# One GNN and mixture-of-experts layer: earlier and later places for sends, combines and a release, and padding written behind each expert's last token

## The reference

```python
x = x + gnn(layernorm(x), src, dst, edge_weight)      # x: 3125 nodes x 256
x = x + ffn(layernorm(x))
# gnn: support = x @ weight; out = segment_sum(support[src] * edge_weight, dst) + bias   (53125 edges)
# ffn, per token: logits = x @ Wg + bg over 8 experts; the best 2, softmax over the two logits;
#   out = sum over the two experts e of w_e * (gelu(x @ W1[e] + b1[e]) @ W2[e] + b2[e])   (256 -> 1024 -> 256)
```

## Time and profile before

| what | value |
|---|---|
| runs | 1106.56, 1114.02, 1115.84 us |
| profiled execution | 1100.59 us, span 1098.9 us |
| mean granted TensorE clock | 0.871 of full speed |
| PE busy / POOL busy / DVE busy / ACT busy | 780.1 / 601.0 / 491.4 / 354.1 us |
| DMA | 121,776 packets, 189.21 MB, 172 GB/s |
| SP's queue | 55,068 packets, 67.83 MB |

### The profile page before, as it was taken

One profiled execution on the slowest core, in us unless ns is written; L12 is line 12 of the kernel. 1 busy time (PEld: TensorE's weight loads), 2 busy tenths in 40 slices (PEclk: granted clock), 3 DMA queues, 4 the chain that ended last, 5 costly groups with the idle time before them and its releaser, 6 DMA issues.

```text
span 1098.9 us, 15759 instructions
## 1 busy us (share of the span) xinstructions
PE 780.1 (71%) x5365; PEld 752.2 (68%) x5365; DVE 491.4 (45%) x1345; ACT 354.1 (32%) x642; POOL 601.0 (55%) x611
## 2 busy tenths in 40 slices
PE   1216376942778899785598957994699986689993
PEld 0216376932768789685588947994689986689892
DVE  6203122440114458472127714670245688476752
ACT  5102001011123144332024603450236464257761
POOL 5575664537646765747566674047456645304543
PEclk9999999956668798888599967996789999699997
DMA  7956466845456568856447755456457674556732
GB/s 209 304 178 162 124 173 171 209 119 161 135 154 207 158 202 232 233 143 186 118 150 240 222 171 187 125 149 168 124 166 236 188 228 139 162 163 173 204 76 39
DMA packets 121776, 189.21 MB, mean 172 GB/s; under 512 B 20684, under 2 KB 94027, under 8 KB 121568
## 3 DMA queue, kind: packets, MB, share of 16 engines
q0 software_dynamic: 34752, 69.40, 23.4%
q1 hardware_dynamic: 55068, 67.83, 21.0%
q10 hardware_dynamic: 31876, 50.97, 15.1%
HBM read 134.81 MB, written 53.24 MB: 171 GB/s over the span
## 4 chain that ended last, share of the span: by engine, by line
PE 49%; issue 18%; DVE 12%; another core or an unknown queue 9%; DMA 4%; ACT 3%; POOL 2%; DVEq 1%; SPq 1%; ACTq 0%; POOLq 0%
PE ps_agg L911 16%; PE ps_o L1054 14%; PE ps_h L1039 14%; DVE w_lo L1267 2%; POOL y_d L674 1%; DVE h_lo L1485 1%; PE ps_g L977 1%; PE ps_y L1025 1%; ACT hf L831 1%; DMA yg<-y_d 1%; DMA xe_int<-in_src 1%; DMA G<-xn_d,src_t 1%; DMA y_d<-yr,pos_i 1%; PE ps_m L968 1%
## 5 line engine op out<-in xcount | busy, mean ns | idle before, releaser
L662 POOL DMA_INDIRECT G<-xn_d,src_t x416 | 418.1, 1005 | 245.6 <-issue 118.7
L911 PE MATMUL ps_agg<-S,G 128*128 128x48 f32 x1664 | 257.2, 319 | 81.5 <-issue 35.1
L911 PEld LDWEIGHTS ps_agg<-S,G 128*128 128x128 f32 x1664 | 255.2, 241 | 83.7 <-issue 50.4
L831 ACT ACTIVATE hf<-ps_h,b_t 128x256 f32<-128x256 f32 x272 | 113.5, 468 | 421.1 <-PE ps_h L1039 310.4
L1039 PE MATMUL ps_h<-y_hi,w_hi 128*128 128x256 f32 x544 | 168.4, 310 | 54.5 <-issue 33.8
L1235 DVE TENSOR_TENSOR S<-iota_w,rel_t 128x192 f32<-128x192 f32 x104 | 36.6, 357 | 334.5 <-remote 205.7
L1039 PE MATMUL ps_h<-y_lo,w_hi 128*128 128x256 f32 x544 | 162.0, 298 | 6.8 <-issue 6.8
L1039 PE MATMUL ps_h<-y_hi,w_lo 128*128 128x256 f32 x544 | 161.7, 297 | 2.2 <-issue 2.1
L1485 DVE TENSOR_TENSOR h_lo<-hf,h_hi 128x512 fp32r<-128x512 f32 x136 | 93.4, 692 | 145.7 <-ACT h_hi L834 119.2
L1039 PEld LDWEIGHTS ps_h<-y_hi,w_hi 128*128 128x128 f32 x544 | 113.5, 209 | 61.2 <-issue 45.2
L1054 PE MATMUL ps_o<-w_hi,h_hi 128*128 128x256 f32 x544 | 127.0, 313 | 23.9 <-issue 15.3
(11 more groups left out here) (196 smaller groups left out, 624.2 us busy)
## 6 DMA issues: line engine op xcount, KB each, us to landing
w_raw<-in_L_ffn_W ACTq DMA_DIRECT2D x48, 1024.0 KB
y_d<-fill SPq DMA_DIRECT2D x30, 388.5 KB
yg<-y_d SPq DMA_DIRECT2D x36, 259.0 KB
y_d<-fill SPq DMA_DIRECT2D x32, 259.0 KB
G<-xn_d,src_t POOLq DMA_INDIRECT x416
y_d<-fill SPq DMA_DIRECT2D x48, 129.5 KB
w_raw<-in_L_ffn_W SPq DMA_DIRECT2D x4, 1024.0 KB
r_d<-ost SPq DMA_DIRECT2D x12, 256.0 KB
```

The source lines that it names most:

```text
L662: pool.indirect_dma_start(G[:, k, :], None, xn_d, bass.IndirectOffsetOnAxis(src_t[:, n, c:c + 1], 0)).then_inc(main.gathered[n % NR], 16)
L831: nc.scalar.activation(hf[:, j % 2, m, :], ps_h[:, j % 2, m * T:(m + 1) * T], ACT.Gelu, bias=b1_t[:, e * KH + c:e * KH + c + 1]).then_inc( ...
L911: return nc.tensor.matmul(ps_agg[:, k // GT % 2, m * WIN:(m + 1) * WIN], G[:, k, m * 128:(m + 1) * 128], S[:, k, :], start=start, stop=stop)
```

## The change

Padding: the fill of a set covers only its own tile of each expert, in sets 0 to 2, in one DMA for each tile; the tile behind all is filled at the start. Behind the last chunk's `ch.pos`, DVE copies the counters `run` (the row behind each expert's last token) to `ends_i`, and SP fills 256 rows from there for each expert, and waits for these fills before it loads tile 24. `ROOM` is 14 instead of 13.

Four orders: sends stand at other places among the gathers; two combines more stand in visit 22 and fewer after visit 23, those of set 2 in two parts; DVE does not wait for the stores of the sums; `q.route` is released once first and end tiles are known, and SP waits for `q.rows`, released where `q.route` was.

```diff
-    REACH = [STILL + -(-sum(OVER[:s.index + 1]) // T) for s in SETS]
-    ROOM = REACH[-1]
-    TPE = ROOM - STILL
+    TPE = -(-sum(OVER) // T)
+    ROOM = STILL + TPE + 1
...
-    SEND_AT = [COMPLETE[0] + pairs_beside(CHUNKS[0]) + 2, U0 + 1]
-    SEND_AT += [min(HEAD_U[v] + PAIRS_AT[v] // 2 + (2 if c in [s.last for s in SETS] else 4), NP) for v, c in RANK_AT.items()]
-    assert sorted(SEND_AT) == SEND_AT and SEND_AT[-1] == NP
+    SEND_AT = [2 * (COMPLETE[0] + pairs_beside(CHUNKS[0]) + 2), 2 * (U0 + 1)]
+    SEND_AT += [min(2 * HEAD_U[v] + n, NG) for v, n in zip(RANK_AT, (6, 3, 10, 3, NG, NG))]
+    assert sorted(SEND_AT) == SEND_AT and SEND_AT[-1] == NG
...
-    COMBINE_AT = {AHEAD - 1: 4, AHEAD: 12}
+    COMBINE_AT = {AHEAD - 1: 6, AHEAD: 12}
...
+        def fill_tile(eng, row, done):
+
+            eng.dma_start(y_d[row, :].rearrange("(h p) d -> p h d", p=128), fill[:, :, :]).then_inc(done, 16)
+
         def fill_rows(eng, s, e):
-
-            parts_to = []
-            if s.index < STILL:
-                parts_to.append((s.index, s.index + 1))
-            parts_to.append((REACH[s.index - 1] if s.index else STILL, REACH[s.index] + (s is SETS[-1] and e == X - 1)))
-            for a, z in parts_to:
...
+            row = (e * ROOM + s.index) * T
+            fill_tile(eng, slice(row, row + T), s_fill[s.index])
...
-                if v < 2 * X:
-                    fill_rows(sp, SETS[2 + v // X], v % X)
+                if v < X:
+                    fill_rows(sp, SETS[2], v)
...
+                if v == AHEAD - 1:
+                    sp.wait_ge(s_ends, 1)
+                    for e in range(X):
+                        fill_tile(sp, bass.ds(sp.value_load(ends_i[0:1, e:e + 1], min_val=0, max_val=(X * ROOM - 1) * T), T), s_ends_filled)
                 if v < AHEAD:
                     store_result(v)
+                if v == AHEAD - 1:
+                    sp.wait_ge(s_ends_filled, 16 * X)
...
-            sp.wait_ge(q.route, 1)
+            sp.wait_ge(q.rows, 1)
             row = tile_row(2)
...
-                if c is s.chunks[0]:
-                    pool.wait_ge(s_fill[s.index], filled(s))
+                if c is s.chunks[0] and s.index < STILL:
+                    pool.wait_ge(s_fill[s.index], 16 * X)
...
                 dve.sem_inc(ch.pos, 1)
+                if c is CHUNKS[-1]:
+                    V.tensor_copy(ends_i[:, :], run[0:1, :]).then_inc(s_ends, 1)
...
                 own(V.tensor_copy(end_i[:, :], end_f[0:1, :]))
+                dve.sem_inc(q.route, 1)
...
-                dve.sem_inc(q.route, 1)
+                dve.sem_inc(q.rows, 1)
...
-            combined = (step for s in SETS[:2] for step in combine(s))
+            combined = (step for s in SETS[:STILL] for step in combine(s))
...
-            for _ in combined:
-                pass
+            combine_some(combined_upto(SETS[1]) - sum(COMBINE_AT.values()))
             for s in SETS[:2]:
                 dve.wait_ge(s_combined[s.index], 2 * (s.z - s.a))
-                dve.wait_ge(s_out[s.index], 32 * len(s.chunks))
...
-                if i == 1:
-                    for _ in combine(SETS[2]):
-                        pass
+                if i < 2:
+                    combine_some(BLOCKS - SECOND)
```

More of the change, by code:

```diff
@@ L74, in __init__ @@
     def __init__(self, sem, halves):
-        self.route = sem("s_route")
+        self.route, self.rows = sem("s_route"), sem("s_tile_rows")
         self.tile_in, self.tile_t, self.y_hi, self.y_split, self.meta = (
@@ L243, in gnn_moe_layer @@
         place_i = sb("place_i", [1, NTR], i32)
+        ends_i = sb("ends_i", [1, X], i32)
         slot_ph = sb("slot_ph", [128, TH])
@@ L342, in gnn_moe_layer @@
         s_fill = [sem(f"s_fill{s.index}") for s in SETS]
-        s_none = sem("s_none")
+        s_none, s_ends, s_ends_filled = sem("s_none"), sem("s_ends"), sem("s_ends_filled")
         s_sums, s_kept, s_combined, s_out = ([sem(f"s_{n}{k}") for k in range(STILL)] for n in ("sums", "kept_in", "combined", "out"))
@@ L474, in _ @@
             sp.wait_ge(s_const, 1)
+            fill_tile(sp, slice(X * ROOM * T, X * ROOM * T + T), s_none)
             for k in range(STILL):
@@ L585, in _ @@
                 sp.wait_ge(done, 32)
+            sp.wait_ge(s_none, 16 * (STILL + 1))
             for s in SETS[:STILL]:
@@ L654, in _, with gather_groups @@
             pool.sem_inc(s_go, 1)
-            def gather_pairs(a, z):
-                for n in range(2 * a, 2 * z):
+            def gather_groups(a, z):
+                for n in range(a, z):
                     for c in range(GT):
@@ L707, in _ @@
             for c, a, z in zip(CHUNKS, [0] + SEND_AT, SEND_AT):
-                gather_pairs(a, z)
+                gather_groups(a, z)
                 if c is SETS[STILL].chunks[0]:
-                    pool.wait_ge(s_none, 16 * STILL)
+                    pool.wait_ge(s_none, 16 * (STILL + 1))
                     gather_kept(SETS[0])
@@ L1528, in combine, with combined_upto @@
                         yield
-            combined = (step for s in SETS[:2] for step in combine(s))
+            combined = (step for s in SETS[:STILL] for step in combine(s))
             def combine_some(n):
                 for _ in range(n):
-                    next(combined, None)
+                    next(combined)
+            def combined_upto(s):
+                return sum(2 * (t.z - t.a) for t in SETS[:s.index + 1])
             tile_low(0)
@@ L1604, in _ @@
                             split_low(LOADS[v + 1], which, n)
-                if i == 1:
-                    for _ in combine(SETS[2]):
-                        pass
+                if i < 2:
+                    combine_some(BLOCKS - SECOND)
             results_in(end - 1)
             results_to_add(end - 1)
+            assert not list(combined)
 _INS = ["x", "src", "dst", "edge_weight", "L0_gnn_weight", "L0_gnn_bias", "L0_ffn_Wg", "L0_ffn_bg",
```

## The result

The changed kernel took 1119.2 us in the median of 20 runs, the kernel before 1110.9 us in 20 runs on the same chip. The ratio is 1.0111 with a 95% interval of 1.0077 to 1.0146: some 12 us slower, where 4.3 us less were forecast. The profiled executions took 1116.96 us (span 1115.3) and 1100.59 us.

The account below looks back on a forecast made before the run. TensorE, busy 71% of the span, was taken as the bound, fed by DVE in the last part. Terms -1 + 6.9 + 2.9 + 1.5 - 8.9 - 2.6 - 3.1 = -4.3 us on 1114.0 gave 1109; range 1095 to 1123.

Parts of the forecast that it names:

- The sends: Moved sends among the gathers: +6.9 us waiting for group 59, +2.9 at the lower clock, 0 for chunks 2 and 5.
- a term put at nothing in the first paragraph: TensorE's idle stretches without a named releaser, like 506.0 to 536.7 us: untouched by the diff, counted as noise.
- the wait for group 59: TensorE, after group 58 in visit 6: a new wait of 7.2 us for a gather, net +6.9 us.
- the unnamed stretches change by over 10 us in sum: Sign that the prediction is wrong: TensorE's idle stretches without a named releaser change by over 10 us together.
- The filled ends: Visit 22, eight fills before tile 24's load: they slow a weight load ScalarE waits for, +1.5 us (0 to +14.5).
- some 3 us of cover: Before tile 24: TensorE's idling for `route` covers a 2 us slide of tile 23, with some 3 us left.
- the early `route`: Tile 24: bounds released before the rest of the tables, so TensorE begins it at 934.0, 4.9 us sooner.
- the rival that let it run to 14.5: Slower rival: end fills and weight load fight for the engines from 908 to 921 us; 1123 us, chance 0.12.
- The tail's orders: Tail: DVE's dropped wait with early `route` -8.9 us, less lower clock -2.6, set 2's combines in two parts -3.1.
- The fills: Padding fills, 72 tiles fewer: less DMA traffic off the path, -1 us (bounds -4 and 0).
- The second rival: Fills' traffic counted everywhere: loads and gathers land sooner, some unnamed stretches shrink by some 5; 1095 us, chance 0.09.
- The chance of 0.10 for slower: Whole kernel: overall chance of a slower result, against 0.30 faster and 0.60 same; half of the last rival's chance.

Follow-up runs that it names:

- 0.9978: The changed kernel with its sends put back at groups 26, 30, 58, 62, 82, 90, 104, 104: 1097.9 us, ratio 0.9978 to the kernel before.
- The same edit: Kernel before with chunk 3's send behind group 64, chunk 5's behind 93, and the tail's three changed orders: ratio 0.9687, on another chip 0.9864.

## Why the prediction was wrong

**The sends.** This is the step that failed. The forecast was +6.9 us of wait and +2.9 at the lower clock, with nothing for chunks 2 and 5. The wait came (6.04 us), and so did the clock (0.51 from 491 to 501 us). But the sends cost 25 us alone (1.0226), or 15 us as the difference between 1.0111 and 0.9978. What failed is a term put at nothing in the first paragraph: "The diff touches nothing in them; I leave them in the sum as they are". These stretches go with the series of gathers that the diff rearranges: with half of the gathers they are nearly gone, and with shorter series they are shorter. The series at tile 7 began 3 us earlier and ended 2 us later (40 DMAs for 36), the slow issue beside it grew from 28 to 34 us, and the wait for group 59 with its lower clock held tile 7 back until its first half ran into that stretch. Tile 7 grew by 18.7 us, of which the named wait is 6, and tile 16, with group 89's four gathers in its series, by 6.7. A view of TensorE's waits from tile 0's turn to tile 17's shows the growth under another name than the one that the prediction watched:

```profile
PE ps_h L1039 <- ACT hf L831: 10.4, 6, 5.6
PE ps_h L1039 <- ACT hf L831: 37.8, 5, 16.8
```

The first is the kernel before, the second the changed one. TensorE's rows named "issue" sum to 104.2 us before and 94.8 after, so by that name alone the prediction's sign, "the unnamed stretches change by over 10 us in sum", was not met. With the waits for ScalarE's late gelus counted to the same stretches they grew by 18 us. Of the 15 to 25 us that the sends cost, the forecast had 9.8; the other 5 to 15 are what it put at nothing. Why ScalarE and TensorE issue late is open.

**The filled ends.** The +1.5 us were too small. Tile 24's load slid by 4.1 us, not 2, and "some 3 us of cover" was not there: tile 23 took 4.0 us longer, and the early `route`, which the forecast counted in full, had used the 10.07 us that were to cover it (4.38 were left with the orders alone, 1.55 in the changed kernel). ScalarE's wait grew by 2.4 us. The price is 4 to 6.5 us; the rival that let it run to 14.5 did not occur.

**The tail's orders.** Forecast -8.9, -2.6 and -3.1, so -14.6. Tiles 24 to 27 fell by 10.8 us with the orders alone, and the runs say -9 us (-4 to -14). The mechanism was right: the rows at 10.60, 10.07 and 3.15 us changed as said, and set 2's -3.1 came to -3.2. The size was off by a third in the first two terms: of TensorE's 10.07 and 5.10 us 8.7 were left, where -8.9 would leave 6.3:

```profile
941.86 0.58 PE L1039 MATMUL ps_h<-y_hi,w_hi 128*128 128x256 f32 x1 [4.38 <-issue]
955.10 0.80 PE L1054 MATMUL ps_o<-w_hi,h_hi 128*128 128x256 f32 x2 [4.28 <-DVE ost L1490]
```

(PE of the kernel with the tail's orders alone, against the earlier trace rows.)

**The fills.** -1 us, from traffic: no run showed a gain, and none could resolve 1 us. The second rival, traffic counted everywhere, had 0.09 and did not happen: the slow issue stayed, at a DMA share of 0.43.

**The sum as measured**: sends +15 to +25, padding +4 to +6.5, orders -9; from +10 to +22 us, and 12 was measured. The chance of 0.10 for slower was low because the only mechanism I gave it was the weight load.

## What to carry to other kernels

A stretch of idling with no releaser named is not noise until something shows that it is: look which queue is busy without a pause beside it, and whether the edit lengthens that. Moving gathers behind a blocking send lengthens the burst that follows the block, and on a chip with the slow issue the same sends were faster with *less* look-ahead (1.0000 for 1.0226). Look at the other engines in such a stretch too: a wait with a name can be another engine's share of the same trouble. The same edit gave 0.9687 on one chip and 0.9864 on another: run the disputed edit on more than one chip before explaining it.

## What was not expected of the hardware

The kernel before took 921 us in the median on one chip and 1103 to 1114 us on three others, with GpSimd's gathers issued equally fast (1032 ns each in the mean on the one, with chunk 2's send moved, and 1005 ns in the kernel before; 1.25 us apart on both). On the three, from 21 to 33 us into a long series of indirect DMAs until it ends, TensorE issues a matmul only every 0.7 to 2.8 us with no releaser named, or waits for a ScalarE that is itself up to 15.4 us late. Leaving out half of the gathers removes nearly all of this (901.8 us on one of the three). What resource it is stays open; that two engines show it speaks against a cause inside TensorE alone. The traffic for instructions doesn't tell them apart, it is the same row on the page of both:

```profile
q8 instruction: 43, 0.70, 0.3%
```

The 24 gathers of kept results (833 to 873 us in the kernel before) bring no slow issue, although their series lasts 40 us. Nor was it tried whether a pause inside a series, in place of a shorter one, ends it.
